# TensorE waits for the first matmul of a stage ahead of its third or fourth, in six stages of each half

## The reference

```python
xn = layernorm(x)
# gated linear attention branch
u = xn @ up_w.T;  gate = xn @ gate_w.T                  # 256 -> 512
shift = silu(causal_conv4(u) + conv_b)
q, k = shift @ q_w.T, shift @ k_w.T                     # 512 -> 64
v = sigmoid(u @ ig_w1.T @ ig_w2.T + ig_b2) * u
g = softplus(shift @ g_w.T + g_b);  tau = sigmoid(shift @ tau_w.T + tau_b)
kn = k / max(norm(k), eps) * g ** tau
o = gla_chunk_scan(q / 8, kn, v, -g * tau) + shift * residual_weight
xg = o * silu(gate)
attn = (xg * rsqrt(mean(xg^2) + eps) * norm_weight) @ down_w.T      # 512 -> 256
# ternary feed-forward branch, weights are -1, 0, 1
h = silu(xn @ w1.T * s1) * (xn @ w2.T * s2)             # 256 -> 1024
h = gelu(h @ h1.T * sh1);  h = gelu(h @ h2.T * sh2)     # 1024 -> 1024
out = x + attn + h @ w3.T * s3                          # 1024 -> 256
```

## Time and profile before

| | before |
|---|---|
| device time, median of 3 runs | 2059.82 us (2059.46 to 2060.64) |
| the profiled execution: device time | 2058.4 us |
| its span, first to last instruction | 2056.5 us |
| TensorE matmul busy | 1984.1 us (96%), 17218 instructions |
| VectorE busy | 1573.9 us (77%) |
| ScalarE busy | 1262.3 us (61%) |
| GpSimd busy | 75.1 us (4%) |
| granted TensorE clock | 1.00 of full speed over the span |
| `h1`, one operand (`hid0h`): 2048 matmuls | mean 280 ns each |
| TensorE's waits in the loop | 17 on `hid1l`, 18.7 us |

### The profile page before, as it was taken

How to read it: one execution, slowest core, us unless ns; L and a number is a source line. 1 busy time by engine, 2 the same in 40 slices (tenths; PEclk the granted TensorE clock), 3 DMA queues, 4 the chain that set the end, 5 groups by cost and what they waited for, 6 DMA issues and landing times.

```text
span 2056.5 us, 46221 instructions
## 1 busy us (share of the span) xinstructions
PE 1984.1 (96%) x17218; PEld 1965.2 (96%) x17218; DVE 1573.9 (77%) x4242; ACT 1262.3 (61%) x2495; POOL 75.1 (4%) x104
## 2 busy tenths in 40 slices
PE   0999999999999999999999999999999999999998
PEld 0999999999999999999999999999999999999998
DVE  7787778877777877777877788777778777778776
ACT  5665656666556666566656566665566665666564
POOL 0000000000000000000000000000000000000000
PEclk9999999999999999999999999999999999999999
DMA  8000000000000000000000000000000000000000
GB/s 291 7 11 12 11 6 6 11 11 11 12 1 11 12 11 11 11 1 12 11 12 11 6 6 11 11 11 12 1 11 12 11 11 11 1 12 11 12 7 7
DMA packets 23358, 34.18 MB, mean 17 GB/s; under 512 B 2945, under 2 KB 19713, under 8 KB 23186
## 3 DMA queue, kind: packets, MB, share of 16 engines
q1 hardware_dynamic: 23186, 31.46, 4.6%
HBM read 23.07 MB, written 8.39 MB: 15 GB/s over the span
## 4 chain that ended last, share of the span: by engine, by line
PE 65%; issue 28%; DVE 3%; ACT 2%; POOL 1%; SPq 1%; DMA 1%; POOLq 0%; DVEq 0%; ACTq 0%
PE fb L355 44%; PE ab L355 17%; PE ab L523 1%; POOL rkn L336 1%; PE ab L405 1%; PE ab L489 1%; DVE hid1l L807 1%; PE fb L601 1%; POOL rms L340 1%; DVE att L1063 0%; ACT wwhole L649 0%; SPq L263 0%; PE ab L467 0%; DVE shift L918 0%; DMA shift<-stage_w 0%
## 5 line engine op out<-in xcount | busy, mean ns | idle before, releaser
L355 PE MATMUL fb<-hid1h,wwhole 128*128 128x256 f32 x2048 | 491.3, 283 | 19.7 <-DVE hid1l L807 18.7
L355 PE MATMUL fb<-hid1l,wwhole 128*128 128x256 f32 x2048 | 483.8, 279 | 0.0
L355 PE MATMUL fb<-hid0h,wwhole 128*128 128x256 f32 x2048 | 481.5, 280 | 0.0
L355 PE MATMUL fb<-hid0l,wwhole 128*128 128x256 f32 x2048 | 478.8, 278 | 0.0
L355 PEld LDWEIGHTS fb<-hid1h,wwhole 128*128 128x128 f32 x2048 | 384.3, 188 | 26.7 <-issue 24.5
L355 PEld LDWEIGHTS fb<-hid1l,wwhole 128*128 128x128 f32 x2048 | 384.5, 188 | 0.0
L355 PEld LDWEIGHTS fb<-hid0l,wwhole 128*128 128x128 f32 x2048 | 384.4, 188 | 0.0
L355 PEld LDWEIGHTS fb<-hid0h,wwhole 128*128 128x128 f32 x2048 | 384.3, 188 | 0.0
L757 ACT ACTIVATE raw<-fb,sh_s 128x256 f32<-128x256 f32 x512 | 213.8, 469 | 259.9 <-PE fb L355 254.8
L355 PE MATMUL fb<-xnth,wwhole 128*128 128x256 f32 x1024 | 239.1, 277 | 0.0
L355 PE MATMUL fb<-xntl,wwhole 128*128 128x256 f32 x1024 | 238.9, 277 | 0.0
(11 more groups left out here) (206 smaller groups left out, 4577.9 us busy)
## 6 DMA issues: line engine op xcount, KB each, us to landing
xin<-x SPq DMA_DIRECT2D x32, 256.0 KB, 2.8
out<-xin SPq DMA_DIRECT2D x32, 256.0 KB, 2.2
stage_more<-stage_w SPq DMA_DIRECT2D x6, 512.0 KB, 7.2
sgate<-stage_w SPq DMA_DIRECT2D x4, 512.0 KB, 4.3
shift<-stage_w SPq DMA_DIRECT2D x4, 512.0 KB, 5.1
v<-stage_w SPq DMA_DIRECT2D x4, 512.0 KB, 5.5
raw<-stage_w SPq DMA_DIRECT2D x3, 512.0 KB, 6.0
mixed<-stage_w SPq DMA_DIRECT2D x3, 512.0 KB, 8.4
```

The lines of the kernel that those rows point to most:

```text
L355: mm = pe.matmul(o, a, b, start=start and i == 0, stop=stop and i == len(pairs) - 1)
```

## The change

`wide` gets two new arguments. With `pace`, the matmul number 0 of a stage increments a new semaphore `paced_mm`, and ahead of the matmul number `PACED[stage]` of the same stage TensorE waits for that increment. `done` says how many matmuls of the stage earlier calls have issued. The stages are up, `proj`, `h1`, `h2`, `w3` and down; each is paced once in a half, at its start. In `h1` and `h2` the counted matmuls belong to the first output block, in `w3` to the first weight tile.

```diff
+PACED = {"up": 3, "proj": 2, "h1": 2, "h2": 3, "w3": 2, "down": 3}
@@
+        paced_mm = sig("paced_mm", len(PACED))
@@
-            def wide(o, pairs, start=True, stop=True):
+            def wide(o, pairs, start=True, stop=True, pace=None, done=0):
 
                 for i, (a, b) in enumerate(pairs):
+                    if pace and done + i == PACED[pace[1]]:
+                        pe.wait_ge(paced_mm.sem, paced_mm.at(pace[0], list(PACED).index(pace[1]) + 1))
                     mm = pe.matmul(o, a, b, start=start and i == 0, stop=stop and i == len(pairs) - 1)
+                    if pace and done + i == 0:
+                        mm.then_inc(paced_mm.sem, 1)
                 return mm
@@
-                        mm = wide(ab[b][:, (m % 2) * N:(m % 2 + 1) * N], pairs)
+                        mm = wide(ab[b][:, (m % 2) * N:(m % 2 + 1) * N], pairs, pace=(me, "up") if m == 0 else None)
@@
-                    mm = wide(ab[2][:, j * N:(j + 1) * N], pairs)
+                    mm = wide(ab[2][:, j * N:(j + 1) * N], pairs, pace=(me, "proj") if j == 0 else None)
@@
-                                      [(wb, a) for a in parts(exact, ih[:, k, :], il[:, k, :])], start=(k == 0), stop=(k == FB - 1))
+                                      [(wb, a) for a in parts(exact, ih[:, k, :], il[:, k, :])], start=(k == 0), stop=(k == FB - 1),
+                                      pace=(me, name) if m == 0 else None, done=2 * k)
@@
-                                  start=(k == 0), stop=(k == FB - 1))
+                                  start=(k == 0), stop=(k == FB - 1), pace=(me, "w3") if k == 0 else None, done=2 * c)
@@
-                    mm = wide(ab[3][:, c * H:(c + 1) * H], pairs)
+                    mm = wide(ab[3][:, c * H:(c + 1) * H], pairs, pace=(me, "down") if c == 0 else None)
```

## The result

The changed kernel takes 2078.85 us (2077.92 to 2079.49), the kernel before, run beside it, 2060.23 us (2059.46 to 2060.64): the ratio is 1.0087, with the interval 1.0075 to 1.0099. It is slower by 18.6 us. The forecast was 2053.3 with a range up to 2070; rival D, "no place locks", had been given 2081 and a chance of 0.12. It is the one that comes nearest: of the six places only `w3` locks, in 30 halves of 32.

What follows compares the result with a forecast made beforehand. TensorE's matmul order and spacing (113 or 118 ns) was taken as the bound. With all six places locked, -2.6, -5.9, +0.6, +2.4 and -1.0 made -6.5 us: 2051.9 profiled, 2053.3 median, range 2046 to 2070.

Steps and rivals of the forecast that it cites:

- rival D: All six stages: no place locks on the fast spacing, the stops only cost; +21 us, 2081, chance 0.12.
- That the order of the matmuls sets the time, and that two spacings exist.: TensorE, busy 96% of the span: its matmul streams set the time, each keeping 113 or 118 ns spacing.
- The cost of one stop: Head of each stage: later matmuls start 0.07 to 0.20 us later, 0.81 us per half, 26 us if all on the path.
- the bound from below: All stops: a signal costing nothing inside one engine makes each 0.04 us cheaper, 7.7 us less in all.
- Where it is hidden: Second halves: stops in `proj`, `h1` and the start of `h2` disappear in a 1.3 us wait on VectorE.
- Whether a stop leads to the fast spacing is the unknown of the case: All six stages: each place expected to go one way in all 32 halves; which way, the trace can't say.
- first halves up to the 13th matmul of `h2`: Up to there 0.29 us shorter in the 9 first halves with slow `h1`, nothing in 7: -2.6 us.
- rest of `h2` in first halves: `h2` behind its 13th matmul: keeps the fast spacing without a real stop, 16 x -0.37 = -5.9 us.
- second halves up to the resumption: Bound by VectorE's 38.16 us; only up's first twelve matmuls come 0.04 us later: +0.6 us.
- rival A: First halves: all lock, but `h2`'s 13th matmul still waits and its rest restarts slow; -0.6 us, 2059.2, chance 0.18.
- B: More than the sum: stages behind a locked one inherit its spacing, or second halves resume fast; 2045 to 2050, chance 0.13.
- rival C: Slower, some places do not lock; +6.0 us, 2066 if only `h1` and `h2` lock; chance 0.21.

Runs made afterwards that it cites:

- E8: Against the kernel before: only `w3` has the stop, ahead of its third matmul; 2064.45 against 2061.32 us, ratio 1.001.
- E5: Against the kernel before: only `proj`, `h1`, `h2` have the stop, in second halves alone; 2061.4 against 2060.87 us, ratio 1.0003.
- E4: Against the kernel before: only up, `w3` and down have the stop; 2070.72 against 2060.87 us, ratio 1.0052.
- E7: Against the kernel before: only `h1` has the stop, ahead of its third matmul; 2064.87 against 2061.32 us, ratio 1.0014.
- E1: Changed kernel with all six stops moved: ahead of the second matmul in first halves, the fifth in second halves; 2090.21 us in one run.
- E2: Changed kernel with counts exchanged: up, `h2`, down stop ahead of the third matmul, `proj`, `h1`, `w3` ahead of the fourth; 2085.69 us in one run.
- E6: Kernel before plus narrow (16-column) matmuls ahead of the second output block of `h1` and `h2`, two in first halves, six in second; 2071.62 us in one run.
- E10: Kernel before plus two narrow matmuls of 64 moving columns inside each of the streams of all six stages; 2085.25 against 2061.33 us, ratio 1.0114.
- E3: Kernel before plus two narrow (16-column) matmuls ahead of each of the six stages, no stop; 2089.26 against 2060.87 us, ratio 1.0138.
- E11: Against the kernel before: only `proj`, `h1`, `h2` have the stop, in first halves alone; 2071.04 against 2059.93 us, ratio 1.005.
- E9: Kernel before plus one narrow matmul ahead of the second output block, in `h1` of first halves and `h2` of all; 2063.67 against 2061.33 us, ratio 1.001.

## Why the prediction was wrong

Right, by its own steps:
- *That the order of the matmuls sets the time, and that two spacings exist.* The whole difference lies in TensorE's stages (19.2 of 19.5 us), and 113 and 118 ns are the only lasting spacings of `h1`, `h2` and `w3` in the changed kernel too, at full clock (`proj` and down average 118 to 120).
- *The cost of one stop.* Predicted 0.08 for up, 0.20 for `proj`, 0.19 for `h1` and `w3`, 0.08 for `h2`, 0.07 for down, 0.81 in a half. Measured 0.09, 0.18, 0.21, 0.21 (E8), 0.09, 0.08: 0.86. The estimate from the consumer's 0.04 us and the 0.20 behind a resumption was good to 0.02 us each, and the long stages show that it is repeatable (the third matmul of `h1` starts 0.420 to 0.424 us after the first in all 32 halves); the bound from below, 0.04 less per stop, was not needed.
- *Where it is hidden.* Second halves hide `proj`, `h1` and `h2` completely (E5, +0.5 us); they resume at 38.23 us after their start instead of 38.15, and those 0.08 are the stop in up (38.24 with it in E4, 38.15 without it in E5), of which the prediction had 0.04. First halves behave as rival D had it: the 13th matmul of `h2` starts at 37.52 us, 0.56 later than behind a slow `h1` and 0.87 later than behind a fast one (D: 0.55 and 0.86). `w3` and down hide nothing anywhere (E4).

Wrong: the step "Whether a stop leads to the fast spacing is the unknown of the case ... I expect each place to go one way in all 32 halves", and what the forecast made of it, that all six go the fast way. The first part held for five places: `h1`, up, `proj` and down are the same in all 32 halves, `w3` in 30; `h2` goes one way in 27 and the other in 5. The second did not: four of the six go the slow way always and `h2` nearly always. So the terms of the sum that were gains became losses:

| term | forecast | measured |
|---|---|---|
| `h1`, in one half in which it was slow before | -0.36 us | +0.21 us |
| first halves up to the 13th matmul of `h2` | -2.6 us | +11.0 us |
| rest of `h2` in first halves | -5.9 us | -1.1 us |
| second halves up to the resumption | +0.6 us | +1.1 us |
| rest of `h2` in second halves | 0 | +1.1 us |
| `w3` | +2.4 us | +4.3 us |
| down | -1.0 us | +2.9 us |

(From the second row on the terms are sums over all halves of a kind; the measured ones, from the two profiled executions, add up to 19 us.) The fifth row is the same matter of chance as before the change, 5 fast halves instead of 8. The forecast had priced the slow way as rival D at +21 us. The change came to +18.6; the largest difference is the one place that did lock: D had `w3` at +6.9 us, where it measured 16 x (0.16 + 0.11) = +4.3.

The argument for it was thin and can now be sized. Fast resumptions were 10 of 28 in the trace, a third (2 of 4 at earlier matmuls of `h2`, and 8 of 24 at the 13th, all eight in second halves, and none of the 8 first halves with a wait), and nothing excluded that a repeatable stop falls on the slow side each time. With a third for each place, and the places taken as independent, both long stages are fast in one case of nine and `h1` is slow in two of three. The forecast, A and B, which all need a fast `h1`, had 0.67 together. The prediction took "each place goes one way" for "each goes the good way"; that its rival D came within 2.4 us is the merit of its prices, not of its odds. In rival C the decision had been put in the right place ("`h1`'s 0.55 must exceed its 0.19"): `h1` never got its 0.55, in the change or with the stop alone (E7), one matmul earlier (E1) or one later (E2).

Not decided: whether the forecast's 5.9 us for the rest of `h2` would have come with a fast `h1`, or rival A. No run has the paced `h2` behind a fast `h1`. What E4, E5 and E8 show is the case without the stop in `h2`: there a fast `h1` in a first half is followed by a wait of 0.09 us, as in the earlier trace rows, and a slow rest in all but one of them (E5). Nor is it known what selects the spacing at all, and so why the stop in `h1` leads to 118 ns each time.

The Trainium skill ("TensorE: Matmul & The Clock Gate", Back-to-back issue gap) gives the formula that the prediction used, columns / 2.4 + 2.5 ns, which would be an estimate of 109 ns here. The prediction read it as the spacing of a stream; the section itself calls it the gap of an isolated matmul and says that in a stream of weight loads and matmuls both set the spacing. By the prediction's reading the change costs its stops alone, which is what it did but for `w3` and the fast halves of `h1` that were lost. The trace of the changed kernel does not agree with the figure, as its fp32 streams run at 113 and 118 ns (3.63 us for 32, and 0.12 us steps behind the stops).

## What to carry to other kernels

With matmuls of this form a stop of TensorE on its own first matmul cost 0.32 us at the second, 0.2 at the third, 0.1 at the fourth and nothing at the fifth; half of the 0.2 is the slower step behind the stop. Where two outcomes of a stream lie 5 ns apart and the trace shows both, count how often each comes, separately for each kind of place, and give the forecast one factor for each place that must go well. And before a gain ahead of a wait is counted, look whether the half resumes at a fixed distance from its start: if so, neither the gain nor the cost reaches the end.

## What the runs showed of the hardware

- The spacing of a stream of fp32 matmuls (128x128 weights, 256 columns) has two values, 113 and 118 ns, holds over a hundred matmuls and more, and can change in mid-stream behind narrow matmuls: in `h1` from slow to fast behind two (5 of 8) or six (8 of 9) with 256 moving columns (E6), and from fast to slow behind two with 64 (E10, 5 of 5). Two at the head of a stage leave `h1` slow in 32 halves of 32, but `w3` is fast in 25 (E3).
- It differs where nothing was edited: with stops in `w3` alone `h1` is fast in 19 halves of 32 instead of 9 (E8), with stops in first halves alone `h1` is fast in none of the 16 second ones and the rest of `h2` in none instead of 8 (E11). That the edits did this is not shown, as each kernel was profiled once.
- In E9, in two second halves, matmuls behind the wait of `h2` were 213 ns apart for a part of it, though the wait, 1.15 us, was as long in the other second halves (1.14 to 1.17). The granted clock is 1.00 ahead of it, 0.70 in the 1.03 us behind it and 0.88 in the 10.3 us after that. The spacing is that of the lower level, 1.2 GHz; the half is 1.5 us longer for it. TensorE's timeline, with the wait that released it, and the windows (us, then busy us and count of PE, PEld, DVE, ACT, POOL, then clock):

```profile
529.57 0.36 PE L358 MATMUL fb<-hid1h,wwhole 128*128 128x256 f32 x1 [1.15 <-DVE hid1l L811]
...
530.00 0.41 PE L358 MATMUL fb<-hid1l,wwhole 128*128 128x256 f32 x1
530.22 0.41 PE L355 MATMUL fb<-hid1h,combh 128*16 128x256 f32 x1
530.43 0.41 PE L358 MATMUL fb<-hid1h,wwhole 128*128 128x256 f32 x1
```

```profile
529.57:530.60 1.03, 1.03 (x6) 0.96 (x7) 1.03 (x3) 0.00 (x0) 0.00 (x0) 0.70 0.00 0
531.00:541.30 10.30, 10.30 (x80) 10.30 (x79) 5.26 (x17) 3.25 (x7) 0.69 (x1) 0.88 0.01 2
```

Why it is these two halves and no others is open.
